# Linear attention with layers in the background: QA2 and what follows it start at another step

## The reference

```python
x = x + 0.5 * quant(layernorm(x))      # QA: int8 rows, 256 x 256 weight
x = x + linear_attention(layernorm(x)) # 16 heads of 128, 4 key/value heads
x = x + 0.5 * quant(layernorm(x))      # QB
x = x + 0.5 * routed(layernorm(x))     # FA: the 128 best tokens of a batch through an MLP
x = x + attention(layernorm(x))        # softmax, 16 heads
x = x + 0.5 * routed(layernorm(x))     # FB
```

```python
def quant(x):
    x_scale = max(max|x| of the row / 127, 1e-12); x_q = clip(round(x / x_scale))
    return (x_q @ w_q.T) * x_scale * w_scale + bias
def linear_attention(x):
    q, k, v = x @ Wq.T + bq, x @ Wk.T + bk, x @ Wv.T + bv
    sq, sk = elu(q) + 1, elu(k) + 1
    kv = einsum('bhsd,bhse->bhde', sk, v); norm = sq . sk.sum(over tokens)
    return ((sq @ kv) / (norm + 1e-6)) @ Wo.T
def routed(x):
    logits = x @ Wr + br; the k = 128 largest of 1024 tokens
    x[tokens] += softmax(weights) * (gelu(x[tokens] @ W1 + b1) @ W2 + b2)
```

## Time and profile before

| | us |
|---|---|
| median of three runs | 3441.98 |
| lowest and highest | 3441.32, 3443.99 |
| profiled execution, device time | 3439.03 |
| its span, first to last instruction | 3437.3 |
| mean granted TensorE clock | 0.993 |
| busy: PE, DVE, ACT, POOL | 3336.6, 2671.8, 2042.7, 1059.2 |
| share of the span | 97%, 78%, 59%, 31% |

### The profile page before, as it was taken

One profiled execution on the slowest core, in us unless ns is written; L12 is line 12 of the kernel. 1 busy time (PEld: TensorE's weight loads), 2 busy tenths in 40 slices (PEclk: granted clock), 3 DMA queues, 4 the chain that ended last, 5 costly groups with the idle time before them and its releaser, 6 DMA issues.

```text
span 3437.3 us, 53015 instructions
## 1 busy us (share of the span) xinstructions
PE 3336.6 (97%) x19523; PEld 2854.1 (83%) x19526; DVE 2671.8 (78%) x5155; ACT 2042.7 (59%) x3733; POOL 1059.2 (31%) x1293
## 2 busy tenths in 40 slices
PE   6899999999999999999999999999999999999997
PEld 4788888778888888888888888888888888888885
DVE  6899996778877778867888677886788767876776
ACT  4777777665556565555555656556555565556553
POOL 4887767522122122122121312212212121212112
PEclk9999999999999999999999999999999999999999
DMA  2222112200000000000000110000000010000000
GB/s 86 88 77 62 59 56 84 62 15 13 13 25 25 13 13 13 15 24 25 15 15 13 31 43 15 13 16 26 23 13 15 18 30 26 16 19 29 28 19 21
DMA packets 98528, 104.24 MB, mean 30 GB/s; under 512 B 10336, under 2 KB 88800, under 8 KB 98144
## 3 DMA queue, kind: packets, MB, share of 16 engines
q1 hardware_dynamic: 98272, 100.85, 9.7%
HBM read 87.18 MB, written 13.63 MB: 29 GB/s over the span
## 4 chain that ended last, share of the span: by engine, by line
PE 72%; DVE 5%; ACT 3%; issue 0%; POOL 0%; DVEq 0%; ACTq 0%; POOLq 0%
PE at_ps_job L2042 12%; PE at_ps_job L35 7%; PE at_ps_job L37 7%; PE at_ps_job L36 7%; PE at_ps_o L35 6%; PE at_ps_o L37 6%; PE at_ps_o L36 6%; PE at_ps_s L35 6%; PE at_ps_s L36 6%; PE at_ps_s L37 6%; DVE at_neg_max L1969 1%; ACT x_resident L1793 1%; DVE at_probT_lo L1836 1%; PE at_ps_job L656 1%; DVE li_wkv_lo L1867 0%; ACT at_probT_hi L1752 0%
## 5 line engine op out<-in xcount | busy, mean ns | idle before, releaser
L1752 ACT ACTIVATE at_probT_hi<-at_ps_job 128x512 fp32r<-128x512 f32 x1024 | 611.7, 598 | 889.1 <-PE at_ps_job L2042 886.8
L1836 DVE TENSOR_TENSOR at_probT_lo<-at_ps_job,at_probT_hi 128x512 fp32r<-128x512 f32 x1024 | 702.8, 686 | 273.0 <-ACT at_probT_hi L1752 262.5
L1793 ACT ACTIVATE x_resident<-at_ps_s,at_neg_max 128x1024 f32<-128x1024 f32 x512 | 570.9, 1115 | 149.5 <-DVE at_neg_max L1969 144.7
L1727 POOL TENSOR_TENSOR li_wkv_hi<-li_bkv,ch_cols 128x256 fp32r<-128x256 f32 x252 | 154.4, 613 | 1608.2 <-PE at_ps_job L37 1557.4
L1969 DVE TENSOR_REDUCE at_neg_max<-at_ps_s 128x1 f32<-128x1024 f32 x512 | 622.1, 1215 | 5.2
L2042 PE MATMUL at_ps_job<-ident,x_resident 128*128 128x128 f32 x4096 | 613.8, 272 | 4.7 <-DVE at_probT_lo L1836 3.0
L2042 PEld LDWEIGHTS at_ps_job<-ident,x_resident 128*128 128x128 f32 x4096 | 495.9, 140 | 97.6 <-issue 7.3
L35 PE MATMUL at_ps_o<-at_probT_hi,at_v_lo 128*128 128x512 f32 x1024 | 446.3, 436 | 7.5 <-DVE li_wkv_lo L1867 6.5
L35 PE MATMUL at_ps_s<-at_k_hi,at_q_lo 128*128 128x512 f32 x1024 | 445.1, 435 | 0.0
L37 PE MATMUL at_ps_o<-at_probT_lo,at_v_hi 128*128 128x512 f32 x1024 | 404.7, 395 | 0.0
L36 PE MATMUL at_ps_s<-at_k_hi,at_q_hi 128*128 128x512 f32 x1024 | 402.0, 393 | 0.0
(11 more groups left out here) (358 smaller groups left out, 7443.1 us busy)
## 6 DMA issues: line engine op xcount, KB each, us to landing
li_bkv<-attn_w SPq DMA_DIRECT2D x256, 128.0 KB, 2.3
li_bkv<-mlp_w SPq DMA_DIRECT2D x112, 128.0 KB, 2.3
li_wo_hi<-li_wo_kept SPq DMA_DIRECT2D x24, 256.0 KB, 2.6
li_wo_lo<-li_wo_kept SPq DMA_DIRECT2D x24, 256.0 KB, 3.0
li_wq_hi<-li_wq_kept SPq DMA_DIRECT2D x48, 128.0 KB, 2.1
li_wq_lo<-li_wq_kept SPq DMA_DIRECT2D x48, 128.0 KB, 2.3
x_resident<-x SPq DMA_DIRECT2D x4, 1024.0 KB, 12.7
out<-x_resident SPq DMA_DIRECT2D x4, 1024.0 KB, 4.9
```

What stands on the lines that cost most here:

```text
L1727: nc.gpsimd.tensor_tensor(hi, src, none, ALU.add).then_inc(s_wh[part], 1)
L1752: nc.scalar.activation(ph[:, i // TC, 4 * half:4 * half + 4, (i % TC) * P:(i % TC + 1) * P], c.turned_bank(2 * TB * u + 2 * i + half), ACT ...
L1793: nc.scalar.activation(prob[:, slot % 2, :], ps_s[slot % 2][:], ACT.Exp, bias=nmax[:, slot:slot + 1], accum_out=rsum[:, u % 2, slot:slot + ...
L1836: nc.vector.tensor_tensor(pl[at], c.turned_bank(2 * TB * u + 2 * i + half), ph[at].bitcast(F32), ALU.subtract).then_inc(s_pl, 1)
```

## The change

One number in the chain of the linear stage's plan, the earliest step of the third batch's quantised layer:

```diff
@@ -971,7 +971,7 @@
     rows, sums = linear_rows()
     BEGIN, END = NORM_FIRST[0] - 6, LOOP * B
     plan = Plan(BEGIN, END + LAG + 2, lambda t: rows.get(t, []),
-                [("QA", 1, -17), ("QA", 2, 0), ("QA", 3, 0), ("QB", 0, LOOP + LAG + 2), ("FA", 0, 0), ("X", 0, 3 * LOOP + 1)], [], BANKS, step_claims)
+                [("QA", 1, -17), ("QA", 2, 9), ("QA", 3, 0), ("QB", 0, LOOP + LAG + 2), ("FA", 0, 0), ("X", 0, 3 * LOOP + 1)], [], BANKS, step_claims)
     made, high, by_dve = plan.made, plan.high, plan.by_dve
     kv_time = {}
     for t in range(BEGIN, END):
```

## The result

| us | before | after |
|---|---|---|
| median of 20 runs | 3440.84 | 3448.82 |
| profiled execution, device time (span) | 3439.03 (3437.3) | 3449.80 (3448.1) |
| linear stage: steps 2, 9, 15, 18 begin at | 91.9, 129.7, 155.7, 170.0 | 93.4, 122.4, 147.8, 169.7 |
| steps 28, 41, 49 begin at | 217.6, 283.8, 317.5 | 220.0, 289.8, 324.0 |
| softmax attention's first product | 669.96 | 679.47 |

The ratio is 1.0024, with a 95% interval of 1.0018 to 1.0030: 8.0 us slower. The 3448.82 is inside the range of 3437.5 to 3450.5 and 4.3 us over the predicted 3444.5.

What follows compares the result with a forecast made beforehand. VectorE's f was taken to set the pace in some linear-stage steps, TensorE in the rest. Terms 1.4 (steps 2 to 48) - 0.5 + 1.0 + 0.6 gave +2.5 us on profiled 3439.03, 3 under the median: 3444.5; range 3437.5 to 3450.5.

Steps and rivals of the forecast that it cites:

- steps 2 to 14: Linear stage: VectorE work leaves steps 2 to 8, -7.3 us; statistics enter steps 9 to 11, -0.8 more.
- Steps 15 to 17: Linear stage, seven claims each: VectorE's added work makes TensorE wait 3.8, 2.1 and 0.1 us; +6.3.
- a half-speed stretch in 15 to 22: Sign that the forecast is wrong: TensorE at half speed somewhere in linear-stage steps 15 to 22.
- The slower rival: Late f in 16 to 17 and 30 to 34, two half-speed stretches, dear pairs, later adds: +9.8, 3451.8 us; chance 10%.
- Steps 18 to 27: Linear stage, TensorE-bound: late ScalarE work taken as 0, QT and QP add 1.4; step 28 at 217.0, +1.2.
- Steps 28 to 40: QA3's statistics join the layer norm's; waits of 0.5 to 2.8 us in 30 to 38; step 49 at 318.2, +1.3.
- From step 49 to the attention: Rest of the linear stage: gelu block -0.5, W2 weight splits +1.0, X0's last eviction +0.6.
- M2: W2 weight splits move onto even steps, some with `kv_lo`; one and a half more 0.69 us waits: +1.0, ends 0 and 2.
- The gelu block: Its 1.42 us wait no longer follows a MADE copy on ScalarE; a second place gives it back: -0.5.
- With unchanged length: Sign that the forecast is right: the attention stage starts 1 to 4 us later and lasts as long as before.
- Hardly does what it says: Everything after step 28 only shifts; steps 2 to 27 net -0.6, the rest 0: 3441.4 us; 86% together with the forecast.
- The faster one: Moved work finds room in steps 13 to 17, keeping the gain of 2 to 14: 3438.5 us; 4% for over 0.2%.

Runs made afterwards that it cites:

- e6: The changed kernel with the bias added four steps later (s = 9 to 12, not 5 to 8) in every quantised layer: 3440.15 us.
- e5: The changed kernel with QA2's and QA3's bias added on 8 of 256 columns only, the rest left out: 3442.63 us.
- e7: The kernel before with the bias added four steps later (s = 9 to 12) in every quantised layer: 3435.86 us.
- e9: The kernel before with the bias in s = 9 to 12 and QA3's earliest step 28, QA2 not moved: 3438.17 us.
- e1: The kernel before with QB0 starting at step 46, so QB0, FA0 and X0 stand one step later: 3443.35 us (+3.0).
- e2: The kernel before with QA3's earliest step 28; QA3, QB0, FA0 and X0 stand as in the changed kernel: 3445.61 us (+5.3).
- e12: e6 with QA2's four maxima taken over 8 of each tile's 256 columns: 3439.43 us.
- e11: The kernel before with FA0's earliest step 64, so FA0 and X0 stand one step later and QB0 stays: 3442.49 us (+2.0).

## Why the prediction was right or wrong

**Right in mechanism, and to the tenth by luck: steps 2 to 14.** The 3.03 us gap and its half-speed stretch went, step 9 came at 122.4 (said: 122.4), step 15 at 147.8 (said: 147.6). But two errors cancel in this. After's step 2 began 1.5 us later than before's, behind a half-speed stretch from 88.3 to 91.7 that before's profile does not have and the forecast did not look for. Steps 2 to 8 then took 29.0 us, not the 30.5 of the forecast, in part because the step-2 wait for GpSimd (1.01 in before), which the forecast had stay, was gone. In e6, which begins step 2 at 90.6, that wait is there (1.00) and the same steps take 30.4.

**Steps 15 to 17, +6.3 said, +7.6 measured.** The waits were 5.3 us, not 6.0; the term lacked the rest, 2.3 us of longer products, of which the half-speed stretch is a part. The prediction had named "a half-speed stretch in 15 to 22" as a sign that it was wrong, and it is there. The slower rival had it, to be decided by a wait over 3 us before step 16: the wait was 3.17, ahead of the output products of step 15 and so earlier than placed, and TensorE fell to 1.2 GHz 0.5 us behind it. Its source is VectorE: f(13) to f(14) took 6.6 us where 5.8 was said, and f(15) to f(16) 7.6 for 7.0. The pairs of steps 13 to 16 took 1.60, 2.17, 1.19 and 1.61, in all 6.6 against 5.2 taken, and the layer norm's pair 0.6 more than before, which had no term at all. The forecast charged a pair with a price of its step in the trace of before, though the bias adds moved with the pairs. This is the step that failed. The row that it calls "0.73 alone" was not even alone, as the last section shows.

The Trainium skill (SBUF — State Buffer, "Who interferes with whom") has VectorE and GpSimd exclude each other on the ports that they share. By that rule the prediction had 7.6 us for the pairs, and would have been the nearer; the trace and e5 to e7 agree with it in kind, and the measured 6.6 with neither figure in size. In one point the trace does not bear out what the prediction took from the page, that the second to start blocks. VectorE's and GpSimd's timelines after:

```profile
248.44 1.79 DVE L104 TENSOR_SCALAR ch_r<-x_resident,ln_mean,ln_rstd 128x256 f32<-128x256 f32 x2
```

```profile
248.47 1.28 POOL L387 TENSOR_TENSOR x_resident<-x_resident,quant_bias_half 128x512 f32<-128x512 f32 x1
```

By these stamps the pair began 0.03 us ahead of the add, and it is the pair that was stretched.

**Steps 18 to 27, +1.2 said, +2.7 measured.** 1.3 us of it came in step 19, 0.74 of that by two waits of 0.36 and 0.38. VectorE's and TensorE's timelines show the first:

```profile
177.38 0.69 DVE L1312 TENSOR_TENSOR li_m_lo<-li_ps,li_m_hi 128x512 fp32r<-128x512 f32 x1 [1.65 <-ACT li_m_hi L1229]
```

```profile
178.13 0.51 PE L35 MATMUL li_ps<-li_wkv_hi,ch_xnT_lo 128*128 128x512 f32 x1 [0.36 <-DVE li_m_lo L1312]
```

VectorE waited 1.65 us for ScalarE's half of a MADE copy, where before it waited 0.21. The prediction put up to 1 us on a late f(19) "if that cover is gone" and took 0; a late ScalarE is what the trace shows, and no run takes ScalarE's new work out of these steps. VectorE's waits for GpSimd's add left steps 20 and 22 as said but did not come back smaller: 1.94, 0.80 and 1.50 at the evictions from 208.9 on, against 1.95, 1.74 and 0.36.

**Steps 28 to 40, +1.0 said, +3.6 measured.** The largest waits came near where they were foretold (2.31 ahead of step 30; 1.78 and 2.02 in 33 and 35), but they are 7.2 us in all, against 6.1 before and 11.1 in the prediction's list; the other 2.5 are busy time. By the prediction's price of 1.7 us a stretch, the third half-speed stretch makes up most of it. The mis-sized term is again the pairs: 1.66, 1.39 and 1.38 before and 1.69, 2.32 and 2.33 after for the layer norm's three. With the adds elsewhere they take 1.74, 1.38 and 1.40 (e6), and QA3 and the tail cost 2.9 us less (e9).

**From step 49 to the attention, +1.1 said, +3.1 measured,** and +3.0 by e1. M2 is the term most mis-sized: its waits are 1.66 and 0.40 for 0.69 and 0.29, an output product behind it waits 0.46 for 0.28, and steps 106 to 117 lost 2.1 where 1.0 was taken, with 0 to 2 as the ends. The gelu block gave back 0.4 (0.94 and 1.53 of waits for 1.42 and 1.43; said: 0.5), but steps 49 to 105 lost 1.1 in all, spread thinly, where nothing else was charged. Steps 118 to 127 gave 1.0 back and the stage's end lost 0.8 (said: 0.6).

**"With unchanged length" for the attention stage** is not refuted. It is 1.3 us longer in after's profile, where its first half-speed stretch is 6.8 us and not 3.4, but this length lies between 2767.6 and 2770.3 us over all the profiles, and e2, whose stage ends with the same layers in the same steps as the changed kernel's, has the shortest. That the attention would start 1 to 4 us later was wrong: it started 9.5 later.

**The rivals.** "Hardly does what it says" is out, since QA3 and the tail move 5.3 us by themselves. The faster one failed as argued. The slower one was nearest in mechanism (pairs dear, half-speed stretches in 15, 33 and 35), its size of 3451.8 a little high; the truth lies between it and the forecast, and 10% was too little for it, because a pair's dearness and a half-speed stretch are not independent mishaps: the dear pairs made the waits behind which the stretches began. The range held because its upper end had the dear pairs and one such stretch in it, not because the sum was sound. What stays open is QA2's remaining 2.0 us with the later bias, and how M2's 2 us divide between GpSimd's order and late f.

## What to carry to other kernels

When background work is moved, price VectorE's instructions by what GpSimd does beside them at the new place, and ask first whether the companion operation can stand elsewhere: moving four adds per layer by four steps gave 4.7 us in the kernel before and 8.4 in the changed one, while no start step tried gained anything. The plan here, which places jobs by steps and bank claims, does not see this cost. Where a forecast makes waits of 2 to 3 us in a stage in which such waits had half-speed stretches behind them, give the stretches a price in the forecast itself, not only in a rival. The length of the wait alone does not tell whether one comes: in step 15 it came behind a wait of 1.90 us in e12 and not behind one of 2.22 in e6.

## What the runs showed of the hardware

- The same code does not run the same way to the microsecond. e1 and e11 have before's instructions up to steps 45 and 63, yet at step 42 stood 3.1 and 2.7 us behind it in their profiles. Of this, 2.6 and 2.7 stand there already at step 2, and e1 and e11 both have a half-speed stretch from about 90.7 that before has not; from step 2 to 28 they gain 1.1 and 1.4, where before's stretch behind step 8 is 6.8 us and theirs 3.4; from 28 to 42 they lose 1.6 and 1.4, with stretches at 254.5 alone (e1) and at 241.0 and 254.7 (e11) for before's at 227.3 and 240.9.
- Among runs of one kernel a lower mean granted clock goes with a longer time: in 33 runs of before on one chip the median was 3441.0 us at 0.993 (14 runs), 3440.3 at 0.994 (14) and 3437.3 at 0.995 (2).
- The changed kernel has five such stretches from step 0 to step 48 in its profile; e6's profile, with the same products in the same steps and waits of at most 2.3 us, has none, in an execution whose clock was the best of its eleven. TensorE's busy time over the span fell from 3341.6 to 3333.8 us with the same 19526 matmuls.
- A pair of 128 x 256 tiles that took 0.72 us with GpSimd quiet took 1.2, 1.6 to 1.9, or up to 2.66 beside its adds, while the 128 x 512 bias adds on GpSimd took 1.26 to 1.37 beside such pairs and no less without them (1.29 beside the pair of 2.66). VectorE bears nearly all of the loss.
- Not every GpSimd instruction does this: the pair of 0.73 at 232.22 ran wholly beside GpSimd's power of eight columns (L119, 232.07 to 233.72), and VectorE's maxima stayed at 0.67 and f at 0.72 to 0.75 whatever GpSimd did.
